# Attention layers 2 and 3 of a four-layer graph network: per-node rows turned on TensorE, ScalarE's order, bank-by-bank copies

## The reference

```python
# layer 2; layer 3 is the same with slope 0.01, no W, no b, and elu at the end
h = x @ W
s_src = h @ a_src
s_dst = h @ a_dst
e = leaky_relu(s_src[edge_src] + s_dst[edge_dst], 0.2)
m = segment_max(e, edge_dst)
ex = exp(e - m[edge_dst])
denom = segment_sum(ex, edge_dst)
alpha = ex / maximum(denom[edge_dst], 1e-09)
out = segment_sum(alpha[:, None] * h[edge_src], edge_dst) + b
```

## Time and profile before

| what | value |
|---|---|
| time, median of 3 runs | 4647.93 us (4639.51 to 4649.34) |
| time of the profiled execution | 4662.39 us |
| its span | 4660.6 us |
| layer 2, from its first to its last VectorE instruction | 3929.9 to 4291.1 us |
| layer 3, the same | 4291.2 to 4654.1 us |
| VectorE busy, share of the span | 3863.6 us, 83% |
| TensorE matmul busy | 3310.9 us, 71% |
| ScalarE busy | 2147.7 us, 46% |

### The profile page before, as it was taken

How to read it: one execution, slowest core, us unless ns; L and a number is a source line. 1 busy time by engine, 2 the same in 40 slices (tenths; PEclk the granted TensorE clock), 3 DMA queues, 4 the chain that set the end, 5 groups by cost and what they waited for, 6 DMA issues and landing times. The chain is left out here.

```text
span 4660.6 us, 66751 instructions
## 1 busy us (share of the span) xinstructions
PE 3310.9 (71%) x20061; PEld 1474.2 (32%) x20061; DVE 3863.6 (83%) x6856; ACT 2147.7 (46%) x4394; POOL 1851.4 (40%) x3682
## 2 busy tenths in 40 slices
PE   5555552026639999999991699999999994166156
PEld 2111111001214444444440344444444442022122
DVE  8999993369968888898888788888888883897898
ACT  6999980047613343343340344444443431075075
POOL 0000006710057777677670466666666663000000
PEclk9999995557869999999995799999999996588589
DMA  4653339976535555555550233333333331544444
GB/s 171 256 208 141 148 142 295 362 254 211 164 83 140 148 142 143 143 142 140 146 141 12 64 91 94 91 94 91 94 91 94 91 94 56 172 176 168 172 152 171
DMA packets 359859, 674.29 MB, mean 145 GB/s; under 512 B 71068, under 2 KB 261724, under 8 KB 347856
## 3 DMA queue, kind: packets, MB, share of 16 engines
q1 hardware_dynamic: 319824, 591.23, 38.6%
q0 software_dynamic: 39680, 78.78, 6.4%
HBM read 398.98 MB, written 270.79 MB: 144 GB/s over the span
## 5 line engine op out<-in xcount | busy, mean ns | idle before, releaser
L670 POOL DMA_INDIRECT arena<-h_table,gidx x808 | 782.6, 969 | 314.6 <-issue 229.7
L818 PE MATMUL banks<-arena,lw 128*65 128x512 f32 (+3 forms) x1050 | 460.6, 595 | 260.8 <-DVE lw L1517 134.3
L1625 DVE TENSOR_TENSOR arena<-banks,arena 128x512 f32<-128x512 f32 x808 | 536.3, 685 | 61.5 <-PE banks L857 43.2
L767 PE MATMUL banks<-arena 128*128 128x500 bf16 x1440 | 366.2, 376 | 278.3 <-DVE arena L1359 271.9
L1745 DVE TENSOR_TENSOR arena<-banks,arena 128x512 f32<-128x512 f32 x808 | 518.8, 684 | 36.6 <-PE banks L967 13.1
L1753 DVE TENSOR_TENSOR arena<-banks,arena 128x512 f32<-128x512 f32 x808 | 516.7, 681 | 1.3 <-PE banks L973 1.3
L1091 ACT ACTIVATE arena<-arena 128x128 bf16<-128x128 f16 x1440 | 455.6, 390 | 40.8 <-DVEq L1290 40.8
L636 POOL DMA_INDIRECT arena<-slots,slot_i x157 | 168.4, 1073 | 746.1 <-DMA slots<-arena 690.2
L1226 ACT ACTIVATE arena<-banks 64x256 f32<-64x256 f32 x808 | 305.8, 378 | 341.2 <-PE banks L999 334.2
L987 PE MATMUL banks<-arena 128*64 128x256 f32 x3232 | 438.5, 392 | 0.5 <-DVE arena L1755 0.5
L973 PE MATMUL banks<-arena 64*128 64x512 f32 x1616 | 436.2, 617 | 1.2 <-DVE arena L1753 0.9
(11 more groups left out here) (287 smaller groups left out, 6329.2 us busy)
## 6 DMA issues: line engine op xcount, KB each, us to landing
arena<-c_flat SPq DMA_DIRECT2D x75, 1562.5 KB, 6.8
slots<-arena SPq DMA_DIRECT2D x90, 1000.0 KB, 3.9
arena<-hs_dump SPq DMA_DIRECT2D x404, 128.0 KB
arena<-mask_rows SPq DMA_DIRECT2D x50, 781.2 KB, 4.3
arena<-in_edge_attr SPq DMA_DIRECT2D x202, 128.0 KB
arena<-placed SPq DMA_DIRECT2D x202, 128.0 KB
xs_dump<-arena SPq DMA_DIRECT2D x202, 128.0 KB
hs_dump<-arena SPq DMA_DIRECT2D x202, 128.0 KB
```

Of the source, the lines that this page charges most:

```text
L670: pool.indirect_dma_start(out=xs[par][:, k * D:(k + 1) * D], out_offset=None, in_=h_table, in_offset=bass.IndirectOffsetOnAxis(ap=gidx[par ...
L767: last = pe.matmul(ps[4 + r % 2][:, 0:BW], row_hot[r][:, k * P:(k + 1) * P], col_hot[r][:, k * BW:(k + 1) * BW], start=k == 0, stop=k == K ...
L818: last = pe.matmul(ps[j][0:rows, 0:n], lw[par][:, 0:rows], ptile[par][:, j * COLS:j * COLS + n], start=isinstance(b, int) and b == 0, stop ...
L1625: V.tensor_tensor(bt[j], ps[5 + j % 2][:, :], h2k[t % 2], ALU.mult).then_inc(bt_sb, 1)
```

## The change

`proj` gets a third extra column and a new order: the source score, the destination score, 64 features, and a column of ones that is written once. `feat`, `score_of` and `other_of` name its parts.

- In layers 2 and 3 the row `brow` is no longer made in `node_stage`; L808 and L1077 stay for layer 0 alone. Of `big_m` only the last 75 columns are filled, and the first of the 25 largest instructions writes `big_m` instead of comparing with it: a TENSOR_SCALAR with one source.
- Shift, slope and difference are worked out on the 25 numbers per partition (`stat`) rather than on full rows. TensorE then turns each column, repeated 128 times by a step of zero, so that it stands as a row on all partitions: 25 transposes for `big_m`, 25 for `brow`. ScalarE copies the first, VectorE the second.
- ScalarE begins with score 0, score 1, exp 0, score 2, score 3 and goes on with exp(b), score(b+3); a score waits for the exp before the last one, not for the last.
- The copy into `lw` falls away in layers 2 and 3; the sums read their weights from `proj`.
- In layers 0, 2 and 3 the last block's sums signal after each bank, ScalarE copies bank by bank, and TensorE turns back each part when it is there.

```diff
-        proj = sb("proj", [P, NB, D + 2])
+        proj = sb("proj", [P, NB, D + 3])
+        feat, score_of, other_of = proj[:, :, 2:D + 2], proj[:, :, 0], proj[:, :, 1]
...
+PV = NB - 1 + -(-N // 512)
...
-                for j in range(NJ):
+                for j in range(NJ) if k == 0 else ():
                     if j == 4:
-                        pe.wait_ge(proj_sb, 4 * (k + 1))
+                        pe.wait_ge(proj_sb, 4)
...
-                        last = pe.matmul(ps[j][0:rows, 0:n], lw[par][:, 0:rows], ptile[par][:, j * COLS:j * COLS + n],
-                                         start=isinstance(b, int) and b == 0, stop=isinstance(b, int) and b == NB - 1)
-                    last.then_inc(pv_done, 1)
+                        last = pe.matmul(ps[j][0:rows, 0:n], proj[:, b, 2:rows + 2] if base else lw[par][:, :], ptile[par][:, j * COLS:j * COLS + n],
+                                         start=b == 0, stop=b == NB - 1)
+                        if b == NB - 1 or j == NJ - 1:
+                            last.then_inc(pv_done, 1)
...
-                pe.wait_ge(ot_sb, NJ * (k + 1))
-                pe.wait_ge(ot_clear, k + 1)
                 for b in range(NB):
+                    if b % 4 == 0:
+                        pe.wait_ge(ot_sb, NJ * k + b // 4 + 1)
+                    if b == NB - 1:
+                        pe.wait_ge(ot_clear, k + 1)
...
-                for j in range(NJ):
-                    n = min(COLS, NP - j * COLS)
-                    pe.wait_ge(diag_sb, NJ * k + j + 1)
-                    pe.matmul(ps[j][:, 0:n], ones[:, :], m_row[:, j * COLS:j * COLS + n], start=True, stop=True).then_inc(mrow_ps, 1)
+                for i in range(2):
+                    pe.wait_ge(stat_sb, 2 * k + i + 1)
+                    for b in range(NB):
+                        bank = NJ * i + b // 4
+                        if bank >= 8 and b % 4 == 0:
+                            pe.wait_ge(mrow_sb, NJ * k + bank - 7)
+                        last = pe.transpose(ps[bank % 8][:, (b % 4) * P:(b % 4 + 1) * P], stat[:, 2 + i, b:b + 1].to_broadcast([P, P]), ident)
+                        if b % 4 == 3 or b == NB - 1:
+                            last.then_inc(mrow_ps, 1)
...
             def evac(k, rows):
-                act.wait_ge(pv_done, NB * (k + 1))
                 for j in range(NJ):
                     n = min(COLS, N - j * COLS)
+                    act.wait_ge(pv_done, PV * k + NB + j)
...
                 def turn(b, r, quarter, half):
                     exp(b, r)
-                    act.wait_ge(exp_ready, b + (NB * (1 + k) + 1))
-                    score(b + 4, r)
-
-                act.wait_ge(mrow_ready, k + 1)
-                for b in range(4):
-                    score(b, b)
-                each(0, NB - 4, turn)
-                for b in range(NB - 4, NB):
+                    act.wait_ge(exp_ready, b + NB * (1 + k))
+                    score(b + 3, (r + 3) % 4)
+
+                act.wait_ge(mrow_sb, NJ * (k + 1))
+                score(0, 0)
+                score(1, 1)
+                exp(0, 0)
+                score(2, 2)
+                score(3, 3)
+                each(1, NB - 3, turn)
+                for b in range(NB - 3, NB):
                     exp(b, b % 4)
...
-            for k in range(3):
-                ran(V.tensor_scalar(vrep[:, k, :], ones[0:D, :], main[:, k, D + 1:D + 2], None, ALU.mult))
+            ran(V.tensor_scalar(vrep[:, :], ones[0:D, :], main[:, 0, 1:2], None, ALU.mult))
...
                 dve.wait_ge(proj_sb, 4 * (k + 1))
-                dve.wait_ge(brow_sb, NJ * (k + 1))
 
             node_stage(0, 0)
+            dve.wait_ge(brow_sb, NJ)
...
-                ran(V.memset(big_m, -BIG))
-                settle()
+                ran(V.memset(big_m[:, N:NP], -BIG))
...
-                    V.scalar_tensor_tensor(big_m[:, 0:N], mask4[r], score(b), big_m[:, 0:N], ALU.subtract, ALU.max,
-                                           reverse0=True).then_inc(maxed, 1)
+                    if b == 0:
+                        V.tensor_scalar(big_m[:, 0:N], mask4[r], proj[:, b, 0:1], -1.0, ALU.subtract, ALU.mult).then_inc(maxed, 1)
+                    else:
+                        V.scalar_tensor_tensor(big_m[:, 0:N], mask4[r], proj[:, b, 0:1], big_m[:, 0:N], ALU.subtract, ALU.max,
+                                               reverse0=True).then_inc(maxed, 1)
...
+                dve.wait_ge(mt_sb, NJ * (k + 1))
+                do(V.tensor_tensor(stat[:, 0, :], mxt[:, :], other_of, ALU.add))
+                do(V.scalar_tensor_tensor(stat[:, 1, :], stat[:, 0, :], slope, stat[:, 0, :], ALU.mult, ALU.max))
+                V.tensor_tensor(stat[:, 2, :], other_of, stat[:, 1, :], ALU.subtract).then_inc(stat_sb, 1)
+                V.scalar_tensor_tensor(stat[:, 3, :], other_of, slope, stat[:, 1, :], ALU.mult, ALU.subtract).then_inc(stat_sb, 1)
+                ran(V.tensor_scalar(slope_score[:, :], score_of, slope, None, ALU.mult))
                 for j in range(NJ):
-                    n = min(4, NB - 4 * j)
-                    dve.wait_ge(mt_sb, NJ * k + j + 1)
-                    V.tensor_tensor(m_row[:, 4 * j * P:(4 * j + n) * P].rearrange("p (b n) -> p b n", b=n),
-                                    ident.rearrange("p (o n) -> p o n", o=1).to_broadcast([P, n, P]),
-                                    mxt[:, 4 * j:4 * j + n].rearrange("p (b o) -> p b o", o=1).to_broadcast([P, n, P]), ALU.mult).then_inc(diag_sb, 1)
-                dve.wait_ge(mrow_sb, NJ * (k + 1))
-
-                do(V.tensor_scalar(slope_score[:, :], proj[:, :, D], slope, None, ALU.mult))
-                do(V.tensor_tensor(m_row, big_m, brow, ALU.add))
-                do(V.scalar_tensor_tensor(m_row, m_row, slope, m_row, ALU.mult, ALU.max))
-                do(V.tensor_tensor(big_m, brow, m_row, ALU.subtract))
-                do(V.scalar_tensor_tensor(brow, brow, slope, m_row, ALU.mult, ALU.subtract))
-                signal(mrow_ready)
+                    n = min(COLS, NP - j * COLS)
+                    dve.wait_ge(mrow_ps, 2 * NJ * k + NJ + j + 1)
+                    ran(V.tensor_copy(out=brow[:, j * COLS:j * COLS + n], in_=ps[(NJ + j) % 8][:, 0:n]))
+                settle()
...
-                    ran(V.scalar_tensor_tensor(ptile[par], ptile[par], 1.0, ctile[par], ALU.min, ALU.mult))
-                    V.tensor_scalar(lw[par][:, 0:D], proj[:, bass.ds(b, 1), 0:D].rearrange("p b f -> p (b f)"), 1.0, None, ALU.mult).then_inc(p_ready, 1)
+                    V.scalar_tensor_tensor(ptile[par], ptile[par], 1.0, ctile[par], ALU.min, ALU.mult).then_inc(p_ready, 1)
```

More of the change, by code:

```diff
@@ L219, in build @@
         slope_score = sb("slope_score", [P, NB])
-        lw = [sb(f"lw{i}", [P, D + 1]) for i in range(2)]
+        lw = [sb(f"lw{i}", [P, D]) for i in range(2)]
         mxt = sb("mxt", [P, NB])
@@ L1321, in _ @@
             ran(V.memset(eps[:, :], EPS))
-            for v in (lw[0], lw[1]):
-                ran(V.memset(v[:, D:D + 1], 1.0))
+            ran(V.memset(proj[:, :, D + 2:D + 3], 1.0))
             dve.wait_ge(consts, 16)
@@ L1486, in l0_top @@
             def l0_top(b, r, between=None):
-                sc = proj[:, bass.ds(b, 1), D:D + 1].rearrange("p b f -> p (b f)")
+                sc = proj[:, b, 0:1]
                 dve.wait_ge(masked, b + 1)
@@ L1552, in _ @@
             a64 = agg[:, :, 0:D]
-            do(V.tensor_tensor(h[:, :, :], a64, proj[:, :, 0:D], ALU.add))
+            do(V.tensor_tensor(h[:, :, :], a64, feat, ALU.add))
             norm(h[:, :, :], h[:, :, :], 2)
@@ L1785, in _ @@
                 slope = (0.2, 0.01)[k]
-                ran(V.memset(big_m, -BIG))
-                settle()
-                def score(b):
-                    return proj[:, bass.ds(b, 1), D:D + 1].rearrange("p b f -> p (b f)")
+                ran(V.memset(big_m[:, N:NP], -BIG))
                 def largest(b, r, quarter, half):
@@ L1795, in largest @@
                     at(maxed, b + NB * k, dve)
[L1796 to L1800 removed]
+                    if b == 0:
[3 more added lines that the diff above has]
+                                               reverse0=True).then_inc(maxed, 1)
+                each(0, NB, largest)
+                settle()
                 for j in range(NJ):
```

42 lines of the change are left out of this document (20 added, 22 removed).

## The result

The changed kernel takes 4576.3 us (median of 4 runs, 4568.71 to 4576.87), the kernel before 4645.12 (4 runs, 4639.51 to 4649.34). The ratio is 0.9849, 95% interval 0.9832 to 0.9866: 69 us less, by the interval 62 to 78. Its profiled execution has a span of 4574.6 us, and layers 2 and 3 together, from the first VectorE instruction of layer 2 to the last of layer 3, take 649.4 us, where they took 724.2.

A forecast was written before the change was run, and what follows sets the result against it. VectorE was taken to bound the loop over 25 blocks, while heads of layers wait for something else. The terms sum to 74.2 us off the 4647.93 us median, giving 4574 us; range 4568 - 7 to 4585 + 9.

The forecast's parts named there:

- end of layer 0: End of layer 0: copying the last sums bank by bank removes TensorE's wait before turning back, 3.1 us.
- no wait and no full fill at the head: Head of layers 2 and 3: the largest scores no longer wait for brow or a full memset, 14.1 us each, 28.2.
- first largest: First of the 25 largest instructions, layers 2 and 3: one source instead of two saves 3.4 us for both, bound 0.
- T0 to rear(0): From the last reduction of largest scores to block 0's first weights: 36.8 and 38.5 us fall to 23.4, saving 28.5.
- rear(0) to rear(2), the first sums: From block 0's weights to block 2's: the first sums take 8.4 us at the low clock as before, no gain counted.
- no lw, rear(2) to rear(24): Steady loop, layers 2 and 3: dropping the lw copy saves 0.10 us in each of 24 turns, 4.8, bound 1.5.
- ends of layers 2 and 3: Ends of layers 2 and 3: copying the last sums bank by bank removes TensorE's wait before turning back, 6.2 us.
- its table load stands behind the wait: ScalarE at loop start: exp 0's 1.3 us table load waits for VectorE's input, in a 13.9 us chain to weights.
- the new order alone costs about 2 us per layer: ScalarE's order at loop start: the new order delays block 0's weights about 2 us per layer, counted inside the total.
- The rival with the transposes at 1.2 GHz: Small prices at their poor end, first part all transposes at 1.2 GHz: 62.9 us saved, 4585 us; chance 20%.
- The good-end rival: Loop start: brow 1.4 us per layer sooner, first sums up to 1.2 per layer faster; 79.4 saved, 4568 us; chance 10%.
- The slow-loop rival: Loop at TensorE's low clock: 11.0 us per turn instead of 6.7, slower than before, 4789 us if all turns; chance 3%.

## Why the prediction was right

The mechanism was right in its main parts; that forecast and median are only 2 us apart is luck, since the terms were less exact than that. It was counted from 4647.93, and with a fourth run the median before is 4645.12. Layers 2 and 3 gave 74.8 us in the two profiles and the end of layer 0 gave 3.3, 78.1 together, where the sum had 74.2. The timed runs show 69 (62 to 78). Where the other 9 us lie is not shown: the timed runs of the kernel before have no trace, and its profiled execution was 17 us slower than their median. The rest of layers 0 and 1, which the change hardly touches, is 7.9 us shorter in the changed kernel's profile; its cause was not looked for.

| term | predicted | measured, both layers |
|---|---|---|
| no wait and no full fill at the head | 28.2 | 28.2 |
| first largest | 3.4 | 3.4 |
| T0 to rear(0) | 28.5 | 33.7 |
| rear(0) to rear(2), the first sums | 0 | 0.2 |
| no lw, rear(2) to rear(24) | 4.8 | 4.3 |
| ends of layers 2 and 3 | 6.2 | 7.8 |
| end of layer 0 | 3.1 | 3.3 |
| projections (not in the sum) | 0 | -2.9 |

- *Head, first largest, lw.* Right in mechanism and size; the runs that put each back, or moved the wait alone, show them one by one. The lw term counted 24 turns at 0.10; 22 of them show it (4.3), and the first ones hang on other waits. The one-source instruction takes 1.77 and 1.85, as the nearest row had it.
- *T0 to rear(0).* Right in direction, 5.2 too small, by two terms. I took `brow` at T0 + 9.5 between two bounds; it was the good bound, T0 + 8.1, in both layers, because the clock stayed up during the transposes (50 in 5.64 us at 1.00, so 2.8 for 25 and not 2.6). Of the ten later profiles that turn the rows, one layer has 9.8 in four and both have 9.9 in one. The other is the step "its table load stands behind the wait": it does not. The load ran directly behind score(1), while mid(0) was still at work, so the chain was 12.6 and not 13.9.
- *ScalarE's order.* The step "the new order alone costs about 2 us per layer" fails. With the table load hidden in both orders, the old order is 0.6 sooner at rear(0) and not measurably different at rear(2).
- *Ends.* The wait is 3.4 to 3.5 and not 3.1, and in layer 3 the clock adds 0.8, which I had left out as a gain. Layer 0's 3.3 is a good case: in five of the ten profiles with the end as changed it would be 1.6, because the clock is lower in the last sums.
- *The rival with the transposes at 1.2 GHz.* The trace spoke against it and still does: after 88 us of idle time TensorE ran 25 transposes and then 50 more, and the window over the latter has the clock at 1.00. That a profile with 0.87 exists shows that the clock's rise varies, not that transposes can't bring it.
- *The good-end rival.* Half of it came true, `brow` at T0 + 8.1. The clock still fell before the first sums: sums(0) take 7.62 and 7.68 us, against 5.47 where TensorE was kept at work, and keeping it at work gave 0.7 us per layer, not 1.2.
- *The slow-loop rival.* Nothing of it: from 4060 to 4210 the clock is 0.97, as it was in the loop before, and it rises during the first sums.
- *Projections.* In layer 3 L801 takes 8.91 us where L800 took 6.63. By the clock records the clock rose 3.2 us after the first transpose of `h` in the kernel before and stayed up for 6.8 us; in the changed one it rose after 4.8 and stayed up for 3.4. Of the thirteen profiles (the kernel before, the changed one and the eleven runs), only two take 25.1 us from layer 3's start to the copy of the projections, the kernel before and the one with its wait moved; the others take 27.3 us or more. So the sum lacks a cost of 2.9 us, at which the prediction had nothing. It may hang on how the kernel ends layer 2, but the end as before alone, on the changed kernel, does not bring it back (28.0 there), and chance is not ruled out with two profiles; the cause stays open.
- *Slips in the working.* 3.9 + 4.1 is 8.0 and not 8.1; the terms of the old order add up to 21.1 and not 21.2; and the spread is called 5 us either way but enters the range as 7 and 9. None moves the forecast, and the result lies inside the range with 5 as well.

## What to carry to other kernels

Find what each stretch waits for, then price the wait and the work apart: of 14.1 us at the head of a layer 10.7 were a wait that could be moved without touching the work. Numbers that belong to a node should be worked out once per node and spread last; and a spread by turning repeated columns costs half of TensorE's time of a product with ones, beside VectorE's part. In a software pipeline more lead is not better: an early instruction of a far block stands ahead of the one that the next engine waits for, and one block less of lead gave 5.3 us a layer at the start without costing anything in the turn.

## What the runs showed of the hardware

- ScalarE's table load for the exponential ran before the wait of its instruction was over: 4049.54 to 4050.82 in the changed kernel, mid(0) ending at 4050.7. The load for the square root (L1067 of the kernel before) did both: behind layer 0's end it ran directly behind ScalarE's last copy, 10 us before VectorE's L1432, on which the square root waits, began; in layer 3 ScalarE idled 20.46 us until that L1432 and loaded then. So it is not the function that decides; what does was not tested.

```profile
1288.07 1.28 ACT L1067 ACT_TABLE_LOAD   x1
...
1298.49 1.82 DVE L1432 TENSOR_REDUCE stat<-tmp_n 128x25 f32<-128x1600 f32 x1
...
4298.92 1.28 ACT L1067 ACT_TABLE_LOAD   x1 [20.46 <-DVE stat L1432]
```

- A short VectorE instruction behind a long one costs less than it lasts: 0.19 us long, 0.098 per turn.
- The changed kernel has the same stretches in layers 2 and 3 on two chips to within the clock's part, but its layer 2 starts at 3919 us on one and at 4432 on the other. A window in layer 1 on both, first the one where it is short (columns as in the earlier trace rows):

```profile
2000.00:2100.00 100.00, 99.10 (x800) 48.16 (x800) 89.56 (x220) 39.59 (x84) 73.56 (x76) 1.00 0.54 143
```

```profile
2000.00:2100.00 100.00, 76.35 (x514) 34.52 (x512) 57.42 (x141) 26.02 (x54) 47.78 (x51) 0.88 0.35 92
```

All engines do less, and the DMA engines move 92 GB/s and not 143. What is late there was not looked into; whoever compares kernels over several chips should compare on the same one, or by stretches.
